# Four opening query slots written out by hand, with their transposes, rotary tables and splits in another order

## The reference

```python
xn = layernorm(x)                              # over 512, no gain
q  = rope(xn @ Wq)      # 32 heads of 128      Wq 512x4096
k  = rope(ctx @ Wk)     # 8 heads, each used by 4 query heads
v  = ctx @ Wv           # 8 heads
a  = softmax(where(mask == 0, -1e9, q k^T / sqrt(128)))   # 64x64 for each batch and head
x  = x + (a @ v) @ Wo                          # Wo 4096x512
x  = x + layernorm(x) @ dequantise(quantise_mxfp4(kernel)) + bias
```

## Time and profile before

| | us |
|---|---|
| median of 3 executions | 1144.09 (1143.73 to 1144.65) |
| profiled execution | 1144.29 |
| its span | 1142.4 |
| PE busy in the span | 1130.7 |
| DVE, ACT, POOL busy | 811.0, 767.5, 628.9 |

### The profile page before, as it was taken

The page is one execution under the profiler, slowest core; times in us unless marked ns, Lnnn a source line. Parts: engine busy times, 40 slices in busy tenths (PEclk is TensorE's granted clock), DMA queues, the critical chain, the costliest instruction groups (busy, mean ns, idle before and its releaser), DMA issues.

```text
span 1142.4 us, 19765 instructions
## 1 busy us (share of the span) xinstructions
PE 1130.7 (99%) x6358; PEld 974.1 (85%) x6358; DVE 811.0 (71%) x1753; ACT 767.5 (67%) x2305; POOL 628.9 (55%) x518
## 2 busy tenths in 40 slices
PE   7999999999999999999999999999999999999999
PEld 5888888888888888888888788888888888888876
DVE  7877777777777777688787766656666665666698
ACT  7866777566676766688766566676766677665663
POOL 7854645365554655579656555544655446545433
PEclk9999999999999999999999999999999999999999
DMA  8211211111111211224212221110201112020001
GB/s 260 84 32 44 74 34 51 33 43 65 40 45 33 61 38 37 93 74 140 55 54 69 84 66 56 36 49 19 84 2 36 47 38 65 11 74 20 1 5 70
DMA packets 51748, 63.47 MB, mean 56 GB/s; under 512 B 8768, under 2 KB 27584, under 8 KB 51648
## 3 DMA queue, kind: packets, MB, share of 16 engines
q1 hardware_dynamic: 50736, 59.86, 17.2%
q0 software_dynamic: 768, 2.10, 0.6%
q10 hardware_dynamic: 144, 0.26, 0.1%
HBM read 58.01 MB, written 4.19 MB: 54 GB/s over the span
## 4 chain that ended last, share of the span: by engine, by line
PE 97%; DMA 1%; DVE 1%; POOL 0%; ACT 0%; issue 0%; SPq 0%; ACTq 0%; DVEq 0%
PE proj L510 15%; PE proj L511 15%; PE proj L512 15%; PE pS L623 9%; PE pO L677 9%; PE pO L678 9%; PE pO L679 9%; PE pV L655 3%; PE pV L656 3%; PE pT L638 2%; PE pO L687 2%; PE proj L524 1%; PE pO L690 1%; PE proj L558 1%; PE proj L564 1%; DMA t<-table,tiny 1%
## 5 line engine op out<-in xcount | busy, mean ns | idle before, releaser
L840 ACT CAST PS<-pT 64x256 fp32r<-64x256 f32 x256 | 93.8, 366 | 293.6 <-PE pV L656 290.3
L1321 POOL TENSOR_TENSOR t<-t,SIN 128x512 f32<-128x512 f32 x124 | 159.7, 1288 | 188.2 <-ACT t L849 187.9
L510 PE MATMUL proj<-XH,QH 128*128 128x512 f32 x508 | 199.6, 393 | 0.0
L512 PE MATMUL proj<-XH,QL 128*128 128x512 f32 x508 | 197.9, 390 | 0.0
L511 PE MATMUL proj<-XL,QH 128*128 128x512 f32 x508 | 197.7, 389 | 0.0
L677 PE MATMUL pO<-OH,AH 128*128 128x512 f32 x432 | 171.4, 397 | 0.0
L678 PE MATMUL pO<-OL,AH 128*128 128x512 f32 x432 | 169.1, 392 | 0.0
L679 PE MATMUL pO<-OH,AL 128*128 128x512 f32 x432 | 168.4, 390 | 0.0
L1325 POOL TENSOR_TENSOR qT<-qT,t 128x512 f32<-128x512 f32 x124 | 159.9, 1289 | 9.7
L1055 DVE TENSOR_TENSOR qT<-proj,COS 128x512 f32<-128x512 f32 x128 | 88.3, 690 | 96.4 <-PE proj L512 57.3
L908 ACT ACTIVATE pS<-pS,tiny 128x64 f32<-128x64 f32 x512 | 142.9, 279 | 9.2 <-DVE tiny L1227 5.0
(11 more groups left out here) (204 smaller groups left out, 2572.3 us busy)
## 6 DMA issues: line engine op xcount, KB each, us to landing
QR<-wq SPq DMA_DIRECT2D x64, 256.0 KB, 2.7
OR<-wo SPq DMA_DIRECT2D x62, 256.0 KB, 3.2
CR<-ctxT SPq DMA_DIRECT2D x16, 256.0 KB, 5.5
KR<-wk SPq DMA_DIRECT2D x16, 256.0 KB, 2.6
UR<-wv SPq DMA_DIRECT2D x16, 256.0 KB, 3.5
acc<-x SPq DMA_DIRECT2D x15, 256.0 KB, 3.5
out<-acc SPq DMA_DIRECT2D x15, 256.0 KB, 2.0
rawx<-x SPq DMA_DIRECT2D x8, 256.0 KB, 2.9
```

The lines of the kernel that those rows point to most:

```text
L510: pe.matmul(dst, lh, rh, start=k == 0, stop=False)
L512: made = pe.matmul(dst, ll, rh, start=False, stop=k == last)
L1321: pool.tensor_tensor(t[:, :], t[:, :], SIN[:, 512 * (s % 2):512 * (s % 2) + 512], ALU.mult).then_inc(g_qs, 1)
```

## The change

The slots 0 to 3 leave the loops (which now begin at `OPENED = 4`) and are written out on each engine. The four queries get banks of their own, directly after x0 to x3; then come x5, x6, k0 and x7. x4 is turned in the bank `pO` instead (`xt_place`). On PE the ropes 0 to 3 move from behind q0 to behind q1; k0 moves ahead of rope 6 and x7; 4 fillers are left instead of 8. q0 and q1 start with their four high by high products, as soon as the high parts are there, and wait for `XL` and `QL` later. x3 is normalised by DVE instead of ACT. On POOL `gather(1)` moves ahead of `inverse("x", 2)`, `low` of the second query weight ahead of `gather(4)`. PE's new order: x0 to x3, 4 fillers, q0, q1, rope 0 to 3, q2, x4, rope 4, q3, x5, rope 5, x6, k0, rope 6, x7, q4, rope 7, q5.

```diff
-X_AT = {t: 4 + t for t in range(4)} | {HALF - 5 + t: 8 + t for t in range(8)}
-ROPE_AT = {1 + t: 4 + t for t in range(4)} | {HALF - 4 + t: 8 + t for t in range(8)}
+X_AT = {HALF - 5 + t: 8 + t for t in range(8)}
+ROPE_AT = {OPENED: 7} | {HALF - 4 + t: 8 + t for t in range(8)}
...
-    out = [("x", T) for T in range(4)]
-    for n in range(FIRST, END):
-        if n == 4:
-            out.append(("k", 0))
+    out = [("x", T) for T in range(4)] + [("q", n) for n in range(OPENED)]
+    out += [("x", 5), ("x", 6), ("k", 0), ("x", 7)]
+    for n in range(OPENED, END):
...
+        def xt_place(T):
+            return pO[:, :] if T == 4 else proj[:, BANK["x", T], :]
...
             def turn_x(T):
-                b = bank(("x", T))
+                if T == 4:
+                    pe.wait_ge(a_cs, 8)
+                else:
+                    bank(("x", T))
...
-                if h == 0 and s % 16 < 2:
-                    pe.wait_ge(v_xl, tiles(s)[3] + 1)
-                if not n:
-
+                if n < 2:
+                    pe.wait_ge(a_xh, 4)
+                    pe.wait_ge(a_hi, n + 1)
                     for k in range(4):
                         pe.matmul(proj[:, b, :], QH[:, h, k], XH[:, k, c], start=k == 0, stop=False)
+                    pe.wait_ge(v_xl, 4)
+                    for k in range(4):
                         pe.matmul(proj[:, b, :], QH[:, h, k], XL[:, k, c], start=False, stop=False)
-                    pe.wait_ge(*lo_made(PLACE["q", 0, 0]))
+                    pe.wait_ge(*lo_made(PLACE["q", 0, n]))
...
+                if h == 0 and s % 16 < 2:
+                    pe.wait_ge(v_xl, tiles(s)[3] + 1)
...
-            keep_warm(8)
-            for n in range(FIRST, END):
+            keep_warm(4)
+            project_q(0)
+            project_q(1)
+            for T in range(4):
+                turn_rope(T)
+            project_q(2)
+            turn_x(4)
+            turn_rope(4)
+            project_q(3)
+            turn_x(5)
+            turn_rope(5)
+            turn_x(6)
+            project_k(0)
+            turn_rope(6)
+            turn_x(7)
+            for n in range(OPENED, END):
...
@@ to_psum @@
+                if (s, t) == (0, 3):
+                    act.wait_ge(v_xl, 5)
...
@@ block.scalar @@
             x_normalise(2)
             x_high(1)
-            x_normalise(3)
             x_high(2)
             high([0])
             x_high(3)
             high([1])
...
+            high(streamed(0)[:3])
+            x_normalise(4)
+            first_ropes()
+            x_normalise(5)
+            high(streamed(0)[3:5])
+            to_psum(0, 1)
+            x_high(4)
+            rope(4)
+            high(streamed(0)[5:])
+            to_psum(0, 2)
+            to_psum(0, 3)
+            x_normalise(6)
+
+            exchange(2)
+            x_high(5)
+            x_high(6)
+            x_normalise(7)
+            rope(5)
+            high(streamed(3))
+            rope(6)
+            x_high(7)
+
+            for n in range(OPENED, END):
...
@@ block.vector @@
+            def turn_q(n):
+                dve.wait_ge(e_qp, n + 1)
+                if not n:
+                    dve.wait_ge(e_xt, 4)
+                    dve.wait_ge(a_cs, 4)
+                times_cos(BANK["q", n], qT[:, 0, :, n, :], 0).then_inc(v_qc, 1)
+                if n in ALONE:
+                    if n > 1:
+                        dve.wait_ge(g_qr, n - 1)
+                    else:
+                        dve.wait_ge(e_ct, 4)
+                        dve.wait_ge(a_cs, 8)
+                    times_sin(BANK["q", n], qx_place(n), 0).then_inc(v_qs, 1)
...
             statistics("x", 3)
             shift_mean(2)
             x_low(0)
-            shift_mean(3)
-            x_low(1)
+
+            normalise("x", 3)
+            for T in range(1, 4):
+                x_low(T)
             statistics("x", 4)
-            x_low(2)
-            x_low(3)
             statistics("x", 5)
             low(PLACE["c", 0, 0])
+            statistics("x", 6)
             shift_mean(4)
             shift_mean(5)
-            statistics("x", 6)
             statistics("x", 7)
-            for n in range(FIRST, END):
+            turn_q(0)
+            shift_mean(6)
+            shift_mean(7)
+            turn_q(1)
+            x_low(4)
+            low(PLACE["c", 0, 1])
+            turn_q(2)
+            low(PLACE["c", 0, 2])
+            low(PLACE["c", 0, 3])
+            turn_q(3)
+            for T in range(5, 8):
+                x_low(T)
+            for n in range(OPENED, END):
...
@@ block.gpsimd @@
             inverse("x", 0)
             gather(0)
             inverse("x", 1)
+            gather(1)
             inverse("x", 2)
-            gather(1)
             inverse("x", 3)
             gather(2)
             gather(3)
             low(PLACE["q", 0, 0])
+            low(PLACE["q", 0, 1])
             gather(4)
             inverse_pair(4)
-            low(PLACE["q", 0, 1])
+            low(PLACE["q", 0, 2])
             gather(5)
-            low(PLACE["q", 0, 2])
             inverse_pair(6)
             low(PLACE["q", 0, 3])
-            for n in range(FIRST, END):
+            rotate_q(0)
+            gather(6)
+            low(PLACE["k", 0, 0])
+            rotate_q(1)
+            gather(7)
+            rotate_q(2)
+            for n in range(OPENED, END):
```

More of the change, by code:

```diff
@@ L520, in bank, with turn @@
                 return BANK[use]
-            def turn(b, src, n):
+            def turn(dst, src, n):
                 for k in range(n):
-                    made = pe.transpose(proj[:, b, 128 * k:128 * k + 128], src[:, 128 * k:128 * k + 128], ident[:, :])
+                    made = pe.transpose(dst[:, 128 * k:128 * k + 128], src[:, 128 * k:128 * k + 128], ident[:, :])
                 return made
             def turn_x(T):
-                b = bank(("x", T))
+                if T == 4:
+                    pe.wait_ge(a_cs, 8)
+                else:
+                    bank(("x", T))
                 if on_act(T):
@@ L742, in _ @@
                     ffn_low(FFN_AT[n - 1])
-                if n in X_AT and X_AT[n] not in (7, 11):
+                if n in X_AT and X_AT[n] != 11:
                     turn_x(X_AT[n])
@@ L771, in x_high @@
                     act.wait_ge(e_qp, 4 * (s - 2) + 4)
-                act.copy(XH[:, :, c], proj[:, BANK["x", T], :].rearrange("p (k t) -> p k t", k=4)).then_inc(a_xh, 1)
+                act.copy(XH[:, :, c], xt_place(T).rearrange("p (k t) -> p k t", k=4)).then_inc(a_xh, 1)
             def x_normalise(T):
@@ L849, in exchange @@
                 act.copy(t[64:128, :], proj[0:64, b, :]).then_inc(a_qx, 1)
-            for n in range(FIRST, END):
-                m = n - 5
[L854 to L862, removed]
+            act.dma_start(acc[:, 0, :], x[0]).then_inc(d_x[0], 16)
+            x_normalise(0)
+            x_normalise(1)
+            x_high(0)
+            x_normalise(2)
+            x_high(1)
+            x_high(2)
+            high([0])
+            x_high(3)
+            high([1])
+            high(streamed(0)[:3])
[19 more added lines that the diff above has]
+            for n in range(OPENED, END):
+                m = n - 5
                 if 0 <= n - 1 < PAIRS and n - 1 not in ALONE:
                     exchange(n - 1)
-                if n == 3:
-                    x_high(7)
                 if n == 5:
@@ L876, in _ @@
                                  proj[:, BANK["w", i], 0:256].rearrange("p (k t) -> p k t", k=2)).then_inc(a_w4, 1)
-                if n - 1 in X_AT and X_AT[n - 1] >= 8:
+                if n - 1 in X_AT:
                     x_high(X_AT[n - 1])
@@ L880, in _ @@
                     f_high(FFN_AT[n - 1])
[L881 to L890, removed]
+                high(streamed(n))
+                if n == 4:
+                    to_psum(1, 0)
+                    to_psum(1, 1)
                 if n in X_AT and X_AT[n] == 15:
                     x_normalise(15)
[L893 to L896, removed]
                 if 0 <= m - 1 < PAIRS and n != PAIRS:
@@ L1164, in _ @@
                     made.then_inc(v_vl, 1)
-                if n - 1 in X_AT and n not in (3, 4):
+                if n - 1 in X_AT:
                     x_low(X_AT[n - 1])
@@ L1196, in _ @@
                     times_cos(BANK["q", n], qT[:, s % 2, :, h, :], s % 2).then_inc(v_qc, 1)
[L1197 to L1214, removed]
                 if n == 4:
@@ L1356, in _ @@
                     inverse("f", FFN_AT[n])
-                lows = [i for i in (streamed(n) if n else ()) if not lo_on_dve(i)]
+                lows = [i for i in streamed(n) if not lo_on_dve(i)]
                 while n % 8 == 0 and lows and STREAM[lows[0]][1] == "o":
@@ L1372, in _ @@
                     low(PLACE["v", 1, 0])
-                for i in lows if n != 3 else ():
+                for i in lows:
                     low(i)
```

42 lines of the change are left out of this document (9 added, 33 removed).

## The result

| | before | after |
|---|---|---|
| median of 21 executions, us | 1144.22 (1143.56 to 1144.82) | 1146.16 (1145.66 to 1147.15) |
| ratio | | 1.0017, 95% interval 1.0011 to 1.0023 |
| profiled execution, its span, us | 1144.29, 1142.4 | 1146.45, 1144.4 |

What follows compares the result with a forecast made beforehand. PE, busy 1130.7 of 1142.4 us, was taken to bound the kernel; gain 2.2 less losses 0.5 + 0.7 + 1.75 + 0.1 gave net +0.9: 1145.2 profiled, median 1145.0 (chance 0.62, own range 1144.3 to 1146.0), stated range 1143.1 to 1146.6.

Steps and rivals of the forecast that it cites:

- The limit: On PE up to q4: q4's start at 31.79 sets the end; at most 2.2 us could be gained.
- The start of q0: In the opening: PE starts q0 at 12.61 instead of 13.62, a gain of 1.01 us.
- L965's spread: DVE's normalisation of x3, judged by the same operation on later tiles: 0.54 to 1.52 us, short end taken.
- Rival 3: In the opening: x3's normalisation waits for POOL, 0.3 us on q0 and on ACT's chain, 1145.3; chance 0.08.
- Rival 4: Before q4: TensorE's clock falls during PE's waits, q4's twelve matmuls take 2.7 us more, 1147.7; chance 0.06.
- Rope 3: On PE before rope 3: its gather lands in time, the 0.80 us wait goes, 0.96 us gained with start roundings.
- The walk through twenty instructions: ACT's chain from the late ropes to exchange 2, reckoned start to start, ending at 27.36.
- The waits of 0.5 and 0.7 us: New PE waits: 0.5 us before x6 for its normalisation, 0.7 before k0 for q2's bank and c3's low part.
- x7 and q4: PE idles 1.75 us before q4, which needs x7's low part by way of ACT and DVE; q4 starts at 32.60.
- Behind q4: After q4: nothing is late, POOL's rotations end before the scores of pair 0 at 38.4.
- Sum: At q4's end, 35.43 instead of 34.52: gain 2.2, loss 0.5 + 0.7 + 1.75 + 0.1, net +0.9 us.
- the wait that this rule gave for x3: In the opening: POOL's gather from 9.83 would hold DVE's normalisation of x3 until 10.82, without changing the sum.

## Why the prediction was right, and where its sizes were off

**The range and the number.** 1146.16 lies in the stated range, but outside the forecast's own narrower one (1144.3 to 1146.0). The waits that it named came, within 0.25 us of their sizes; about 1.1 us of the loss came from two terms that the sum had at nothing, the slow transposes of the opening and slot 64. That the result still fell inside owes more to the width of the range than to the sum.

**The limit.** "So whatever shifts PE's start of q4 (31.79) shifts the end by as much": shown. The 1.60 us at the end of q4 are there unchanged 500 us later.

**The start of q0** failed by 0.62 us (12.61 forecast, 13.23 in the first profile, 12.85 in the second). The step named L965's spread as the risk; that came out at its short end (0.54). What failed is "PE turns it at 10.19, for 0.66, until 10.85": the 0.66 was read from a profile in which the transposes were already fast, and here the 8 took 1.97, the first four 1.12. That is 0.45 us of the 0.62; 0.20 more stand in x2's start (10.39 against 10.19), and 0.14 of these already in POOL's first inverse (4.95 against 4.81 in the kernel before). In the profile with nine fillers, where the spacing was fast, q0 starts at 12.62 and the whole step holds. The list of PE's waits leaves out 0.70 us before x3's transposes (11.33 in the kernel before); it changes no sum, since q0 waits for x3's low part in any case. Rival 3, x3 waiting for POOL, didn't come. Rival 4 named PE's slow pace, but as a fall of the clock before q4: there the twelve products of q4 took 2.85 us, no sign of it. The slow pace that came was the one of the start, and it lasted longer than in the profile read.

**Rope 3.** The wait is gone, but the gain (0.96 with the rounding of starts) belonged mostly to the one execution read the earlier trace rows; in the second profile of the kernel before it would have been 0.22.

**ACT and DVE.** The walk through twenty instructions held: from rope 3 to the exchange's end 8.53 forecast (18.83 to 27.36), 8.66 measured (19.44 to 28.10). The waits of 0.5 and 0.7 us were 0.41 and 0.48.

**x7 and q4.** From the start of x7's transposes to the start of q4 2.10 forecast, 2.04 measured. The 1.75 of the sum counts from 0.35 us behind the transposes' start, where PE could have gone on; counted so, 1.69 were measured, and the 1.45 of the row counts from the end of the last transpose. That k0 had covered it is shown by moving k0 alone (+1.98 us).

**Behind q4.** "Behind it nothing is late" holds up to slot 63 and failed at slot 64 in both profiles of the changed kernel (0.49 and 0.50 us). The cause named here, a conversion on DVE that meets a split on POOL, is shown in the profiles by its removal and by the ends of the eleven conversions, while its part in the medians isn't. What makes the conversion late enough to meet the split is open: ACT waits for a DMA just before it (0.40 us for a context tile at 537), and so it does, for 0.2 to 1.7 us, in all ten profiles in which q4 ends later than in the first profile of the kernel before, and in none of the other three. With only k0 moved it is 0.47.

**Sum.** Forecast +0.9; measured +1.94 in the medians and +2.0 in the spans. Of the second, 0.9 is as forecast, 0.6 the opening, 0.5 slot 64. In the second pair of profiles the difference is 2.5 (1144.0 less 1141.5), about 0.9 as forecast, 0.2 the opening, 0.7 the part of rope 3 that the kernel before didn't have there, 0.5 slot 64. How the medians' 1.94 divides among the last three can't be told from single profiles.

## What to carry to other kernels

A long product that needs nothing new is worth most between the last producer of a chain and its consumer; before it is moved ahead, add up the chain that it hides (transposes, high part, low part and one start: 2.0 us here). If it must go, order the consumer's own products so that those come first which need the shorter chain. And take a wait in one profile as a gain only after a second profile has shown it again: the delay of rope 3 by its DMA was 0.96 us in one execution and 0.22 in the next.

## What the runs showed of the hardware

- TensorE begins at a slow spacing (8 transposes of 128 columns in 1.97 us, against 1.09 in the profile with q4's high parts first, 10.32) and goes over at a time that differs between executions of one kernel: in the changed kernel 8 took 1.97 us in one profile and 1.36 in the other; in the kernel before the first profile was fast from 9.97, and in the second the four of x3 were still slow at 10.94. The granted clock reads 1.00, the level of 2.4 GHz, in each of the first three stretches of 5 us of the kernel before, although its first four transposes took 1.11 us and its third four 0.66, and it reads 1.00 in the same stretches of the changed kernel; the spacing of the matmuls is the better witness.
- A `tensor_scalar` from int32 to uint8 (128x128) on DVE takes 0.22 us by itself. Begun while POOL does a `tensor_tensor` of 128x512 (1.3 us), it is shown long, not late, and ends 0.07 to 0.10 us behind POOL's instruction: so it is in all fourteen cases of the two first profiles in which POOL's instruction had more than 0.2 us left to run, with 0.36 to 1.38 us for the conversion. The Trainium skill, page "SBUF — State Buffer", in its practical consequences, says that whichever of the two issues first keeps the shared port for its whole instruction; these ends agree. A gather on POOL held neither a DVE normalisation (10.00, 0.54 us, the gather from 9.94 to 10.94) nor a conversion (544.48, 0.22 us, the gather from 544.19), so the wait that this rule gave for x3 in the prediction did not come.
